# Edge scatter of a graph network: lines loaded six groups ahead, running base added on VectorE, bin numbers in PSUM and read in pairs

## What is computed

```
x = norm(x + relu(segment_sum(weight * x[src], dst) @ W + b))   # layer 0: by destination
x = norm(x + attention(x, src, dst))                            # layer 1: 4 heads
x = norm(x + two_hops(x, src, dst))                             # layer 2
x = norm(x + radial_convolution(x, weight, attr, src, dst))     # layer 3

# attention: segments are by *source*, values come from the destination
hp  = einsum('nf,hfo->hno', h, w)
e   = leaky_relu(a_src[:, src] + a_dst[:, dst] + fc_b, 0.2)
e   = exp(e - segment_max(e, src)[src])
att = e / segment_sum(e, src)[src]
out = segment_sum(att * hp[:, dst], src).mean(heads) + bias
```

## Time and profile before

| | |
|---|---|
| median of 3 runs | 21488.82 us |
| profiled execution: time, span | 21466.85 us, 21465.2 us |
| engines busy over the span | PE 69%, DVE 64%, POOL 50%, ACT 42% |
| `push_rows` | about 5420 to 10515 us: 5095 us, 6.3 us a group |
| `attend` | about 10540 to 12110 us |
| in `push_rows` | PE 3851 us busy, DVE 2435, ACT 377, POOL 3204 of 5095; granted TensorE clock 0.67 |
| in `attend` (10560 to 12100 us) | PE 1423 us busy, DVE 1328, ACT 1403, POOL 244 of 1540; clock 0.98 |

### The profile page before, as it was taken

The page is one execution under the profiler, slowest core; times in us unless marked ns, Lnnn a source line. Parts: engine busy times, 40 slices in busy tenths (PEclk is TensorE's granted clock), DMA queues, the critical chain, the costliest instruction groups (busy, mean ns, idle before and its releaser), DMA issues. The chain is left out here.

```text
span 21465.2 us, 383453 instructions
## 1 busy us (share of the span) xinstructions
PE 14813.3 (69%) x90401; PEld 11962.1 (56%) x90403; DVE 13756.7 (64%) x34135; ACT 8944.7 (42%) x19931; POOL 10752.2 (50%) x11493
## 2 busy tenths in 40 slices
PE   1322223223677777777799778888887888888887
PEld 1322223222555555555688645555556888888887
DVE  4111111111544444444588689999998999999999
ACT  5511111111000000000399578878885555555554
POOL 4666666665566666666411100000003888888887
PEclk7555555555666666666799799999998999999998
DMA  2111111112111111111255243323332222222223
GB/s 62 14 15 14 14 14 14 14 14 13 49 55 54 55 54 55 55 54 55 50 49 49 28 110 105 105 92 105 105 105 59 45 45 45 45 45 45 45 45 42
DMA packets 2474852, 1092.63 MB, mean 51 GB/s; under 512 B 1948758, under 2 KB 2168119, under 8 KB 2473529
## 3 DMA queue, kind: packets, MB, share of 16 engines
q1 hardware_dynamic: 2045096, 646.79, 14.8%
q0 software_dynamic: 312576, 231.97, 6.7%
q10 hardware_dynamic: 117044, 212.38, 3.4%
HBM read 997.70 MB, written 96.88 MB: 51 GB/s over the span
## 5 line engine op out<-in xcount | busy, mean ns | idle before, releaser
L2814 POOL DMA_INDIRECT conv_far<-conv_rows x3232 | 3074.2, 951 | 2864.1 <-DMA tile_ends<-ends_by_src,window_of_tile 2012.0
L1544 POOL DMA_INDIRECT rows_by_src<-push_row,push_index x3232 | 3210.3, 993 | 1893.0 <-issue 1233.1
L818 POOL DMA_INDIRECT weighted_far<-in_x_dram,weighted_rows x3232 | 3060.9, 947 | 2041.7 <-DMA weighted_rows<-edges_by_dst 1078.0
L896 PE MATMUL weighted_total<-weighted_message,weighted_hot 128*128 128x33 f32 x6464 | 1476.7, 399 | 3580.0 <-ACT weighted_message L920 1695.8
L896 PEld LDWEIGHTS weighted_total<-weighted_message,weighted_hot 128*128 128x128 f32 x6464 | 1424.2, 329 | 3633.4 <-issue 3632.1
L1397 PE MATMUL hop_sums_ps<-hop_hots,place_i 128*96 128x512 bf16 x11904 | 2828.8, 380 | 387.8 <-issue 382.8
L2935 PE MATMUL conv_radial_a<-radial,conv_hidden 128*128 128x256 f32 x6464 | 2663.8, 498 | 374.6 <-DVE conv_products_b L3073 227.3
L1323 DVE TENSOR_SCALAR hop_hots<-hop_wide_iota,hop_nodes 128x512 bf16<-128x512 f16 x10416 | 2866.0, 351 | 3.0 <-PE hop_sums_ps L1397 3.0
L844 DVE TENSOR_TENSOR local_of_edge<-weighted_rows,first_node_by_dst 128x4 f32 (+1 forms) x808 | 131.7, 163 | 4023.1 <-DMA weighted_rows<-edges_by_dst 3589.0
L1632 PE MATMUL push_rank<-push_base,push_first_row 128*128 128x490 f32 x1616 | 1369.2, 944 | 1098.3 <-DVE push_base L1598 797.4
L1397 PEld LDWEIGHTS hop_sums_ps<-hop_hots,place_i 128*96 128x96 bf16 x11904 | 1344.4, 123 | 1385.9 <-issue 475.4
(11 more groups left out here) (364 smaller groups left out, 28609.0 us busy)
## 6 DMA issues: line engine op xcount, KB each, us to landing
hop_line<-sources_of_tiles SPq DMA_DIRECT2D x744, 512.0 KB
push_line<-local_by_group ACTq DMA_DIRECT2D x808, 256.0 KB
conv_weights<-weight_by_group SPq DMA_DIRECT2D x808, 128.0 KB
att_far_all<-rows_by_src SPq DMA_DIRECT2D x880, 80.0 KB
weighted_rows<-edges_by_dst SPq DMA_DIRECT2D x3232, 4.0 KB
weighted_far<-in_x_dram,weighted_rows POOLq DMA_INDIRECT x3232
rows_by_src<-push_row,push_index POOLq DMA_INDIRECT x3232
conv_rows<-edges_by_dst SPq DMA_DIRECT2D x3232, 4.0 KB
```

The lines of the kernel that those rows point to most:

```text
L818: pool.indirect_dma_start(far[s][:, j, :], None, table, bass.IndirectOffsetOnAxis(ap=rows[s][:, j, 0:1].bitcast(I32), axis=0)).then_inc(ga ...
L896: last = pe.matmul(total[:].rearrange("p n c -> p (n c)")[:, bass.ds(at[s % SLOTS * HALVES + j // COLUMNS], width)], hot[b][:, j, :], mess ...
L1544: pool.indirect_dma_start(k.rows_by_src, bass.IndirectOffsetOnAxis(ap=index[s][:, j:j + 1], axis=0), row[s][:, j, :], None).then_inc(writt ...
L2814: pool.indirect_dma_start(far[s][:, j, :], None, k.conv_dram, bass.IndirectOffsetOnAxis(ap=rows[s][:, j, 0:1].bitcast(I32), axis=0)).then_ ...
```

## The change

In `push_rows`:

1. Lines have 8 buffers instead of 4 and are loaded 6 groups ahead instead of 2.
2. The matmul that spread the running base is gone, and with it the wait of TensorE for `base_ready`. The rank group now opens with an `all_ones` bf16 matmul over all 5 columns, and `not_earlier` (-1 where `earlier` is 0) corrects column 0. VectorE adds the base to the ranks in PSUM (128x490), waits for that step, then copies the new base.
3. The 98 bin numbers lie in PSUM, beside the node number, instead of SBUF.

In `attend`: VectorE reads the bin numbers of two groups inside each pair, behind the issue of the one-hots; GpSimd reads two at every second group. Both read 16 at the head of a turn before.

```diff
@@ push_rows
+        LINES, LINES_AHEAD = 2 * SLOTS, 2 * SLOTS - 2
+        def nth_line(i, s):
+            return i * (RING // LINES) + s // LINES
-        line = sb("line", [P, GROUP], SLOTS)
+        line = sb("line", [P, GROUP], LINES)
-        node_ps = ctx.enter_context(nc.psum_tensor("push_node", [P, 512], F32))[:, 0:1]
+        fixed = ctx.enter_context(nc.psum_tensor("push_fixed", [P, 512], F32))
+        node_ps, bin_numbers = fixed[:, 0:1], fixed[:, 1:BINS + 1]
+            dve.tensor_scalar(not_earlier[:], k.before[:], -1.0, None, ALU.add).then_inc(units_set, 1)
@@ mark_bins
-                dve.tensor_tensor(bin_hot[b][:], spread(k.iota[:, 1:BINS + 1], 1, PER),
+                dve.tensor_tensor(bin_hot[b][:], spread(bin_numbers, 1, PER),
                                   spread(src_bin[:, group_columns(i, s)], 2, BINS), ALU.is_equal
@@ VectorE, one_turn
-                    dve.wait_ge(line_in[b], (nth(i, s) + 1) * 16)
+                    dve.wait_ge(line_in[s % LINES], (nth_line(i, s) + 1) * 16)
                     dve.wait_ge(rank_ready[c], half(i, s) + 1)
-                    dve.tensor_copy(base[1 - c][:], rank_ps[c][:, PER, :]).then_inc(base_ready[1 - c], 1)
+                    n_based = steps.step(dve.tensor_tensor(rank_ps[c][:], rank_ps[c][:], spread(base[c][:], 1, PER + 1),
+                                                           ALU.add))
+                    steps.wait(n_based)
+                    n_base = steps.step(dve.tensor_copy(base[1 - c][:], rank_ps[c][:, PER, :]))
@@ TensorE, rank
-                pe.wait_ge(base_ready[c], half(i, s) + 1)
                 if again or s >= 2:
                     pe.wait_ge(rank_taken[c], half(i, s))
-                pe.matmul(rank_ps[c], first_row[:], spread(base[c][:], 1, PER + 1), start=True, stop=False)
                 pe.wait_ge(bins_marked[b], nth(i, s) + 1)
-                for j in range(PER):
+                pe.matmul(rank_ps[c], all_ones[:], spread(bin_hot[b][:, 0, :], 1, PER + 1), start=True, stop=False)
+                pe.matmul(rank_ps[c][:, 0, :], not_earlier[:], bin_hot[b][:, 0, :], start=False, stop=False)
+                for j in range(1, PER):
@@ ScalarE, load_line
-                if again or s >= SLOTS:
-                    act.wait_ge(turned_ready[b], nth(i, s))
+                if again or s >= LINES:
+                    act.wait_ge(turned_ready[s % SLOTS], nth(i, s) - 1)
@@ attend, VectorE, one_pair
                     one_hots(i, q + 1)
                 n_local = None
+                at = None
+                if not (first and q < 2):
+                    at = bins(i * SRC_DEEP + 2 * q - 4, 2)
@@ attend, VectorE, one_turn
-                at = [None] * 4 + [*bins(0, SRC_DEEP - 4)] if first else bins(i * SRC_DEEP - 4, SRC_DEEP)
@@ attend, GpSimd, one_turn
-                at = bins_of(nc, mybir.EngineType.Pool, k, "by_src", i * SRC_DEEP, SRC_DEEP)
                 for s in range(SRC_DEEP):
+                    if s % 2 == 0:
+                        at = bins_of(nc, mybir.EngineType.Pool, k, "by_src", i * SRC_DEEP + s, 2)
```

More of the change, by code:

```diff
@@ L1499, in push_rows @@
         base = sb("base", [P, BINS], 2)
-        first_row = sb("first_row", [P, P], 1)[0]
         earlier, all_ones = sb("earlier", [P, P], 1, BF16)[0], sb("all_ones", [P, P], 1, BF16)[0]
+        not_earlier = sb("not_earlier", [P, P], 1, BF16)[0]
         rank_ps = [ctx.enter_context(nc.psum_tensor(f"push_rank{c}", [P, 512], F32))[:, 0:(PER + 1) * BINS].rearrange(
             "p (j b) -> p j b", b=BINS) for c in range(2)]
-        base_ready, rank_ready, rank_taken = sem("base_ready", 2), sem("rank_ready", 2), sem("rank_taken", 2)
+        rank_ready, rank_taken = sem("rank_ready", 2), sem("rank_taken", 2)
+        base_set = sem("base_set", 1)[0]
         place = sb("place", [P, PER], RING)
@@ L1517, in push_rows @@
         near = ctx.enter_context(nc.psum_tensor("push_near", [P, SLOTS, 512], F32))
-        node_ps = ctx.enter_context(nc.psum_tensor("push_node", [P, 512], F32))[:, 0:1]
+        fixed = ctx.enter_context(nc.psum_tensor("push_fixed", [P, 512], F32))
+        node_ps, bin_numbers = fixed[:, 0:1], fixed[:, 1:BINS + 1]
         cells = ctx.enter_context(nc.psum_tensor("push_cells", [P, 512], F32))
         index_ready, row_ready, written = (sem(n, RING) for n in ("index_ready", "row_ready", "written"))
-        line_in, turned_ready, near_ready, near_copied, bins_marked, bins_counted = (sem(n, SLOTS) for n in (
-            "line_in", "turned_ready", "near_ready", "near_copied", "bins_marked", "bins_counted"))
+        line_in = sem("line_in", LINES)
+        turned_ready, near_ready, near_copied, bins_marked, bins_counted = (sem(n, SLOTS) for n in (
+            "turned_ready", "near_ready", "near_copied", "bins_marked", "bins_counted"))
         dst_ready = sem("dst_ready", RING)
@@ L1560, in _ @@
             dve.tensor_copy(earlier[:], k.before[:]).then_inc(units_set, 1)
-            dve.tensor_copy(first_row[:], k.ident[:, 0:1].broadcast_to([P, P])).then_inc(units_set, 1)
-            dve.tensor_copy(base[0][:], k.src_start[:]).then_inc(base_ready[0], 1)
+            dve.tensor_scalar(not_earlier[:], k.before[:], -1.0, None, ALU.add).then_inc(units_set, 1)
+            dve.tensor_copy(base[0][:], k.src_start[:]).then_inc(base_set, 1)
+            dve.wait_ge(base_set, 1)
             steps.step(dve.memset(k.counts[:], 0.0))
@@ L1569, in _ @@
             steps.step(dve.tensor_copy(node_ps, node[:]))
+            steps.step(dve.tensor_copy(bin_numbers, k.iota[:, 1:BINS + 1]))
             steps.step(dve.tensor_scalar(off_centre[:], k.local[:], (P - 1) / 2, None, ALU.subtract))
@@ L1667, in load_line @@
             def load_line(i, s, again):
-                b = s % SLOTS
-                if again or s >= SLOTS:
-                    act.wait_ge(turned_ready[b], nth(i, s))
+                b = s % LINES
+                if again or s >= LINES:
+                    act.wait_ge(turned_ready[s % SLOTS], nth(i, s) - 1)
                 act.dma_start(line[b][:].unsqueeze(1), k.local_dram[
                     bass.ds(i * RING + s, 1), :].partition_broadcast(P)).then_inc(line_in[b], 16)
-            for s in range(SLOTS // 2):
+            for s in range(LINES_AHEAD):
                 load_line(0, s, False)
@@ L1680, in one_turn @@
                     b = s % SLOTS
-                    ahead = s + SLOTS // 2
+                    ahead = s + LINES_AHEAD
                     if ahead < n:
@@ L2423, in accumulate, with one_pair @@
                 return step(dve.tensor_tensor(sums, sums, part[q % 2][:, g * HEADS * W:(g + 1) * HEADS * W], ALU.add))
-            def one_pair(i, q, first, last, at, n_local):
+            def one_pair(i, q, first, last, n_local):
                 if not (last and q == PAIRS - 1):
@@ L2457, in one_turn @@
                 steps.restart()
-                at = [None] * 4 + [*bins(0, SRC_DEEP - 4)] if first else bins(i * SRC_DEEP - 4, SRC_DEEP)
                 n_local = None
                 for q in range(PAIRS):
-                    pair = at[2 * q:2 * q + 2]
-                    n_local = one_pair(i, q, first, last, None if pair[0] is None else pair, n_local)
+                    n_local = one_pair(i, q, first, last, n_local)
                 wait()
@@ L2568, in one_turn @@
                     pool.tensor_copy(node_short[b][:], node_parts[:].rearrange("p b c t -> p (b c t)")[
-                        :, bass.ds(at[s] * width, width)]).then_inc(b_node_ready[b], 1)
+                        :, bass.ds(at[s % 2] * width, width)]).then_inc(b_node_ready[b], 1)
             pool.wait_ge(parts_made, 1)
```

2 lines of the change are left out of this document (1 added, 1 removed).

## The result

The changed kernel takes 21659.35 us (median of 4 runs, 21629.74 to 21671.01) against 21487.92 before (4 runs): ratio 1.0077 [1.0061, 1.0093], **slower by 0.8%**, 171 us. A second measurement on another chip gave 21627.16 against 21483.92, ratio 1.0065 [1.0048, 1.0082]. The forecast was 21420. The time lies in the range, but on the other side of no change, near the second rival's 21675.

The account below looks back on a forecast made before the run. The prediction took push_rows to be bound by a lock step of GpSimd's DMA runs and TensorE's late-seen completions; -78 + 47 - 35 = -66 us on the 21488.82 median gave 21423, rounded to 21420, range 21120 to 21700.

Parts of the forecast that it names:

- second rival: push_rows: VectorE's longer chain makes GpSimd wait for the index, cycles 21.2 us for three groups; 21675 us, chance 0.22.
- Which stage and which wait: push_rows: no engine full; GpSimd's runs of DMAs and TensorE's completions, seen late, move in lock step.
- the row to watch: push_rows: GpSimd's waits for the index, 346.9 us before; over 500 us after would mean the second rival holds.
- Bin numbers in PSUM, -78: push_rows: marking no longer stretches GpSimd's DMAs, mean 994 to 970 ns; 24 ns x 3232 DMAs, -78 us.
- the run's length adds to every cycle: push_rows: premise of the -78 us, that the DMAs' 24 ns each stand on the path.
- Add on VectorE, +47: push_rows: index 0.7 us later after a release, paid in at most 67 long waits for the index: +47 us.
- still pass or are let through: push_rows: near matmuls, now ending at about 5.1 us of the run, get out before the run needs them at 10.2.
- Base matmul 0.1: push_rows: removing the base matmul from TensorE gives 0.1 us on the path, which the add on VectorE eats.
- lines 0: push_rows: loading lines six ahead costs and gains 0, as no line is late.
- Attention, -35: attend: 55 loads of 16 go, -61 us; 438 loads of two expose 0.06 us a pair, +26; sum -35.
- The closing doubt: push_rows: if held completions depend on TensorE's own fp32 work, the stage could end anywhere down to 4121 us.

Follow-up runs that it names:

- psum_only: The kernel before with only the marking's bin numbers moved from SBUF to PSUM: 21627.98 us, ratio 1.0059.
- add_only: The kernel before with only VectorE's addition, all_ones and not_earlier in place of the base matmul: 21676.62 us, ratio 1.0078.
- delay_only: The kernel before plus an unused VectorE addition of 128x490, TensorE unchanged: 19697.46 us, ratio 0.9994, where nothing is held; again where results are held, 21727.92, ratio 1.0105.

## Why the prediction was wrong

*Which stage and which wait.* Right. The scatter is bound by a lock step between GpSimd's runs and TensorE's held results, and the row to watch was the wait for the index, over 500 us.

*Bin numbers in PSUM, -78.* The failed step. That the DMA shortens came true (994 to 971 ns, forecast 970). The Trainium skill (SBUF: State Buffer, the two separate sides) states that a VectorE instruction with at most one input in SBUF, outside its two-port modes, doesn't contend with GpSimd. The trace agrees: no DMA of psum_only is over 1.1 us long, 227 of before are. Wrong was "the run's length adds to every cycle". The cycle is set by the release, which comes 17.3 us after the run's start with the stretch, without it and with pauses; I had measured it from the run's last DMA (2.0 us), on runs of twelve alone. The runs of eight in the same trace tell the two apart: there it comes 1.6 us after the last DMA's end, and 11.4 to 11.6 after the start in all the kernels. Measured: +112, since the stretch had been a pause that let a rank through. By the table 37 more long cycles at 1.9 us and 95 more runs of eight at 0.43 (12.7 us against two thirds of 18.4) make 111.

*Add on VectorE, +47.* The other failed step. Right in sign, and mis-sized: +160 alone (the lost stretches included), +244 as a mere delay. I counted only runs that already waited for the index (67), and took it for the rest that near and rank "still pass or are let through". That was an assumption without a row. The ranks fail it: those that VectorE takes 10 to 12 us after the start fell from 97 in 225 runs of twelve to 4 in 189 (add_only). The second rival had this mechanism with its price, 21.2 us a cycle (measured 20.7). Its chance, 0.22, was too low for a forecast that rested on an assumption no row bore out.

*Base matmul 0.1, lines 0.* Consistent with -13 for the lines; the matmul's removal alone wasn't tried.

*Attention, -35.* Right: -40 in the profile after, -46 alone.

*The closing doubt*, that the hold has to do with the amount of TensorE's own fp32 work: no. The fp32 matmul of the base, 1369 us in before, is gone, and the last held sum of a run of twelve comes 17.26 us after the start in place of 17.32. (The near matmuls, fp32 too, are in both kernels.)

## What to carry to other kernels

When a stage is a lock step, a shorter instruction is worth something only if the event that closes the cycle moves with it; find what that event is timed from before a saving is booked on it, with two runs of different length if there are any. In such a stage a short pause of the issuing engine can be worth more than the time it takes. And where an unexplained hold sets the pace, measure on more than one chip: here both the gain and the loss of one and the same edit depend on it.

## What the runs showed of the hardware

- Of the chips in these runs one didn't hold TensorE's results at all: 19708.8 us against 21353.62 to 21516.29 for the same kernel, nearly the whole difference in two stages in which indirect DMAs of GpSimd run beside matmuls, the scatter (4293, in delay_only, against 5082 us) and the weighted sum (4040 against 5030). The third such stage, the convolution, takes 5028 against 5031; VectorE is busy 4985 of 5000 us in it. Why chips differ, stays open.
- Where results are held, the last comes out about 1.45 us per indirect DMA after the run began, and in between some come early, the more often when GpSimd has paused for 0.3 us (a rank 10 to 12 us after the start in 56 of 177 runs of twelve, against 2 of 165). What holds them, and why a pause lets some out, stays open.
- A VectorE instruction with two inputs in SBUF stretches a GpSimd DMA beside it: a mean of 1023 ns when each group's marking meets one (chip without holding) against 968 with one input in PSUM.
- A load of two numbers into VectorE's registers (0.53 us) once in each pair of 3.28 us costs 0.02 us of it when it stands behind an instruction of 0.69 us.
